# A five-stage graph network on one Trainium2 core: where 832 single-element scatters are issued, and when the first layer compares its edge keys

## The reference, cut to what matters

```
L0: h = gelu(layernorm(conv(h))) + h  four times, then gelu(conv(h))
    conv: alpha = sum(q[dst]*k[src]) / sqrt(32) in 4 heads; softmax over the edges of a dst;
          out = segment_sum(v[src]*attn) + x @ Ws + bs
L1: a relation layer: src_feat = x_rel[type, src], a softmax over each (type, dst), segment_sum
L2: two GCN layers: out = segment_sum(h[src] * dinv[src] * dinv[dst]) + b, an elu between them
L3: out = leaky(segment_sum(edge_weight * h[src]) + b)
x = layernorm(x + L(x)) after each of L0 to L3
```

## Time and profile before

| | |
|---|---|
| runs | 4928.97, 4922.57 and 10345.03 us, median 4928.97 us |
| profiled execution | 4927.95 us, its span 4926.1 us |
| mean granted clock of PE | 0.741 of full speed |
| busy | PE 3395.7, DVE 2708.5, ACT 1597.4, POOL 3350.3 us |
| indirect DMAs of POOL | 1664 + 416 gathers for L0, 416 for L1, 416 + 416 scatters |

### The profile page before, as it was taken

The page is one execution under the profiler, slowest core; times in us unless marked ns, Lnnn a source line. Parts: engine busy times, 40 slices in busy tenths (PEclk is TensorE's granted clock), DMA queues, the critical chain, the costliest instruction groups (busy, mean ns, idle before and its releaser), DMA issues. The chain is left out here.

```text
span 4926.1 us, 76606 instructions
## 1 busy us (share of the span) xinstructions
PE 3395.7 (69%) x17088; PEld 2562.8 (52%) x17089; DVE 2708.5 (55%) x6617; ACT 1597.4 (32%) x3614; POOL 3350.3 (68%) x3343
## 2 busy tenths in 40 slices
PE   6466766676666666656676688885777756969159
PEld 3366653565535555355564566663767653434124
DVE  7577764666646666556665566655777752111001
ACT  5133332334323333223332355562323312221101
POOL 5177766777767777677776777767777767766720
PEclk6677767778777787777867789895555557989579
DMA  8699946666447675376662766643333202323055
GB/s 262 182 274 273 278 143 183 195 202 204 138 140 217 202 206 158 104 219 203 205 182 83 229 202 202 187 117 86 84 69 82 69 11 91 101 91 97 1 204 198
DMA packets 708257, 784.47 MB, mean 159 GB/s; under 512 B 182494, under 2 KB 585924, under 8 KB 704188
## 3 DMA queue, kind: packets, MB, share of 16 engines
q1 hardware_dynamic: 567932, 478.29, 31.4%
q0 software_dynamic: 139968, 302.44, 22.4%
HBM read 657.83 MB, written 122.47 MB: 158 GB/s over the span
## 5 line engine op out<-in xcount | busy, mean ns | idle before, releaser
L673 POOL DMA_INDIRECT kvconv<-kv_tab,src_all x1664 | 1628.4, 979 | 680.3 <-issue 500.0
L2085 POOL DMA_INDIRECT weights<-of_g,cells_g x416 | 454.8, 1093 | 188.1 <-issue 128.0
L687 POOL DMA_INDIRECT counts<-num_now,ord_now x416 | 432.7, 1040 | 193.1 <-issue 154.1
L673 POOL DMA_INDIRECT rows_r<-rel_tab,idx_r x416 | 421.9, 1014 | 141.1 <-issue 125.0
L673 POOL DMA_INDIRECT kvlast<-kv_tab,src_all x416 | 406.1, 976 | 133.5 <-issue 124.4
L1179 ACT ACTIVATE Sconv<-s8conv 128x512 f32<-128x512 fp8e4 x384 | 240.7, 627 | 354.2 <-PE pA1conv L1135 247.1
L1241 DVE TENSOR_TENSOR msgconv<-kvconv,sm_attEconv 128x512 f32<-128x512 f32 x416 | 285.5, 686 | 83.3 <-PE pA0conv L1135 36.5
L1135 PEld LDWEIGHTS pA0conv<-Sconv,msgconv 128*128 128x128 f32 x1664 | 308.6, 260 | 13.8
L1135 PE MATMUL pA0conv<-Sconv,msgconv 128*128 128x128 f32 x1664 | 308.2, 347 | 0.0
L1169 ACT ACTIVATE STconv<-st8conv 128x512 f32<-128x512 fp8e4 x416 | 257.7, 628 | 106.3 <-DMA st8conv<-st_tab 90.6
L1266 DVE TENSOR_REDUCE sm_alphaconv<-prodbconv 128x16 f32<-128x512 f32 x416 | 283.0, 680 | 2.5 <-DVE sm_exconv L526 0.5
(11 more groups left out here) (634 smaller groups left out, 7853.6 us busy)
## 6 DMA issues: line engine op xcount, KB each, us to landing
qwinconv<-q_tab SPq DMA_DIRECT2D x1664, 64.0 KB
raw_g<-counts SPq DMA_DIRECT2D x50, 896.0 KB, 4.8
hot_g<-weights SPq DMA_DIRECT2D x28, 1600.0 KB, 7.5
weights<-blankconv SPq DMA_DIRECT2D x150, 224.0 KB
kvconv<-kv_tab,src_all POOLq DMA_INDIRECT x1664
st8conv<-st_tab SPq DMA_DIRECT2D x52, 512.0 KB
keyrowconv<-key_tab SPq DMA_DIRECT2D x104, 256.0 KB
s8conv<-s_tab SPq DMA_DIRECT2D x52, 512.0 KB
```

Source lines behind the costliest of these rows:

```text
L673: nc.gpsimd.indirect_dma_start(rows[:, par * TG + t, :], None, tab, bass.IndirectOffsetOnAxis(ap=idx[:, g * TG + t:g * TG + t + 1], axis=0 ...
L687: nc.gpsimd.indirect_dma_start(counts, bass.IndirectOffsetOnAxis(ap=ord_now[:, i:i + 1], axis=0), num_now[:, i:i + 1], None).then_inc(sem( ...
L2085: nc.gpsimd.indirect_dma_start(weights, bass.IndirectOffsetOnAxis(ap=cells[:, i:i + 1], axis=0), of[:, i:i + 1], None).then_inc(sem("heavy ...
```

## The change

- Counts: `MID` 26 to 36, `JOINT` 34 to 46, `DRAIN` 30 to 42, and 46 instead of 28 in `last_joint`. That makes 4 x 82 + 88 = 416, so the relation layer scatters no counts any more: neither 5 after each group nor 58 in its drain.
- Weights: 80 are scattered in the drain of the relation layer, after its last gather, from two small buffers that SP fills at the start of that layer (`cells_r`, `of_r`). The other stages get 42 (n1, was 45), 118 (g1, was 110), 34 (e1, was 36), 118 (g2, was 110) and 24 (n2, was 115).
- First layer: `compare`, `matches` and `take` run 8 turns later against the scores than before; `key_rows` and `part_rows` move with them on SP's queue, and the last group's part comes after `sum_rows` in the drain.
- `tables`: POOL writes the iota first, as soon as DVE has read what stood in `first_b`, and gathers then.

```
-JOINT = 34
-MID = 26
+JOINT = 46
+MID = 36
 PER = MID + JOINT
-DRAIN = 30
-EACH = 5
-COUNTED = [(CONVS - 1) * PER, DRAIN + 28, EACH * (GROUPS - 1), T - (CONVS - 1) * PER - DRAIN - 28 - EACH * (GROUPS - 1)]
-WEIGHED = [45, 110, 36, 110, 115]
-MOST = 72
+COUNTED = [(CONVS - 1) * PER, T - (CONVS - 1) * PER]
+DRAIN = 42
+WEIGHED = [80, 42, 118, 34, 118, 24]
+MOST = max(PER, COUNTED[1])
...
                     def _(pool):
+                        pool.wait_ge(ch, 1)
+                        nc.gpsimd.iota(first_b[:, :], pattern=[[1, T]], base=V0, channel_multiplier=0).then_inc(placed, 1)
                         for g in range(2):
                             gather_group(pool, "c_", 0, g, g, kv_tab, src_all, kv)
-                        pool.wait_ge(keyed, 1)
-                        nc.gpsimd.iota(first_b[:, :], pattern=[[1, T]], base=V0, channel_multiplier=0).then_inc(placed, 1)
...
-                            if marks is not None and not (isinstance(g, int) and g * QG + q < 7):
-                                key_rows(g * QG + q - 5, (q + 1) % 2)
-                            if marks is not None and q == 3 and not (isinstance(g, int) and g < 2):
-                                part_rows(g, par)
+                            if marks is not None and not (isinstance(g, int) and g * QG + q < 15):
+                                key_rows(g * QG + q - 13, (q + 1) % 2)
+                            if marks is not None and q == 5 and not (isinstance(g, int) and g < 3):
+                                part_rows(g - 1, 1 - par)
...
                     if marks is not None:
-                        for n in range(GROUPS * QG - 5, GROUPS * QG):
+                        for n in range(LAST * QG - 5, LAST * QG):
                             key_rows(n, n % 2)
                     sp.wait_ge(sem(tag + "S"), quad(LAST - 1, 0))
                     settle(sp)
                     sum_rows(LAST, 0)
+                    if marks is not None:
+                        part_rows(LAST, 0)
+                        for n in range(LAST * QG, GROUPS * QG):
+                            key_rows(n, n % 2)
...
-                            behind = shifted(g, q, par, -1)
+                            behind = shifted(g, q, par, -QG - 1)
...
-                        if marks is not None and q == 1 and started(g):
-                            take(g - 1)
+                        if marks is not None and q == 1 and not (isinstance(g, int) and g < 2):
+                            take(g - 2)
...
-                        if marks is not None and scored(g):
-                            compare(g, q)
+                        if marks is not None and started(g):
+                            compare(g - 1, q)
...
-                    counts_landed(pool, sum(COUNTED[:2]))
+                    counts_landed(pool, T)
...
                     def group(g, par):
                         gather_group(pool, tag, 0, g, par, rel_tab, idx1, rows)
-                        if g == 0:
-                            pool.wait_ge(sem("ord_in"), 32 * (CONVS + 1))
-                        if g < LAST:
-                            add_counts(pool, EACH, EACH * g)
                     gather_all(pool, group)
-                    counts_landed(pool, sum(COUNTED[:3]))
-                    order_in(pool, sum(COUNTED[:3]), COUNTED[3], "ord_pool")
-                    pool.wait_ge(sem("ord_pool"), 32)
-                    add_counts(pool, COUNTED[3])
+                    pool.wait_ge(sem(tag + "weights"), 32)
+                    add_weights(pool, cells, of, 0, WEIGHED[0])
...
                     scatter_rows(0, 0)
-                    order_in(sp, sum(COUNTED[:2]), COUNTED[2])
+                    sp.dma_start(cells[:, :], weigh_at[:, 0:WEIGHED[0]]).then_inc(sem(tag + "weights"), 16)
+                    sp.dma_start(of[:, :], weigh_of[:, 0:WEIGHED[0]]).then_inc(sem(tag + "weights"), 16)
```

More of the change, by code:

```diff
@@ L94, in recycle @@
     def recycle():
-        kept = [n for n in sems if n.startswith(("rows", "settled", "cells", "ord_in", "filled"))]
+        kept = [n for n in sems if n.startswith(("rows", "settled", "cells", "ord_in", "filled", "heavy"))]
         nc.clear_and_free_semaphores([s for n, s in sems.items() if n not in kept])
@@ L1551, in _, with rel_edges @@
                             parts(b - 1)
-        def rel_edges(sb, pb, acc, rs, deg, dinv_f, dinv_n, type_f, mask, last_mask, cuts, idx1):
+        def rel_edges(sb, pb, acc, rs, deg, dinv_f, dinv_n, cells, of, type_f, mask, last_mask, cuts, idx1):
             tag = "r_"
@@ L2271, in _, with late_layers @@
                         v.tensor_scalar(acc[:, cols], pA[b][:, 0:wide(b)], bias, None, ALU.add)
-        def late_layers(l, acc, deg, dinv_f, dinv_n, rs):
+        def late_layers(l, acc, deg, dinv_f, dinv_n, rs, cells, of):
             with ExitStack() as keep:
@@ L2293, in late_layers @@
                         rel_edges(maker(part, nc.sbuf_tensor, "_r"), maker(part, nc.psum_tensor, "_r"), acc, rs, deg,
-                                  dinv_f, dinv_n, *edges)
+                                  dinv_f, dinv_n, cells, of, *edges)
         def elu_joint(tag, acc, y, low, rows, w, bias, dinv_n, pb, weigh, ahead):
@@ L2421, in last_layers @@
                     norm_joint("n1_", acc, rs, sb, pb, [(wb[:, :], w2[1]), (bias[0][:, :], b2[0])], wa, rows=rows,
-                               scale_n=dinv_n, weigh=weigh(0), ahead=counts_ahead("g1_"))
+                               scale_n=dinv_n, weigh=weigh(1), ahead=counts_ahead("g1_"))
                 scope, sb, pb = part("g1_")
                 with scope:
-                    counted("g1_", raw, full, hot, rows, rooted, acc, sb, pb, weigh(1), rs=rs, build=build)
+                    counted("g1_", raw, full, hot, rows, rooted, acc, sb, pb, weigh(2), rs=rs, build=build)
                 scope, sb, pb = part("e1_")
                 with scope:
-                    elu_joint("e1_", acc, y, low, rows, wb, bias[0][:, 0:1], dinv_n, pb, weigh(2), counts_ahead("g2_"))
+                    elu_joint("e1_", acc, y, low, rows, wb, bias[0][:, 0:1], dinv_n, pb, weigh(3), counts_ahead("g2_"))
                 scope, sb, pb = part("g2_")
                 with scope:
-                    counted("g2_", raw, full, hot, rows, rooted, acc, sb, pb, weigh(3),
+                    counted("g2_", raw, full, hot, rows, rooted, acc, sb, pb, weigh(4),
                             loads=[(wc[:, :], w3), (bias[1][:, :], b2[1]), (bias[2][:, :], b3)])
@@ L2434, in last_layers @@
                 with scope:
-                    norm_joint("n2_", acc, rs, sb, pb, [], wc, rows=rows, shift=bias[1][:, 0:1], weigh=weigh(4),
+                    norm_joint("n2_", acc, rs, sb, pb, [], wc, rows=rows, shift=bias[1][:, 0:1], weigh=weigh(5),
                                ahead=weights_ahead)
@@ L2462, in gnn_kernel @@
             acc = scope.enter_context(nc.sbuf_tensor("acc_late", [P, NPAD + P], f32))
+            cells = scope.enter_context(nc.sbuf_tensor("cells_r", [P, WEIGHED[0]], i32))
+            of = scope.enter_context(nc.sbuf_tensor("of_r", [P, WEIGHED[0]], f32))
             with ExitStack() as part:
                 deg = part.enter_context(nc.sbuf_tensor("deg", [1, NPAD + P], f32))
-                late_layers(CONVS - 1, acc, deg, dinv_f, dinv_n, rs)
+                late_layers(CONVS - 1, acc, deg, dinv_f, dinv_n, rs, cells, of)
                 recycle()
```

## The result

The changed kernel takes 4943.64 us, median of 7 runs (4941.83 to 4952.51), against 4922.57 for the kernel before: ratio 1.0045, interval 1.0036 to 1.0055 (one run of the kernel before, at 10345.03 us, does not count in the ratio). That is 0.45% slower, inside the 2% that the forecast named as no difference, but it is a measured loss where I had expected a gain: 4914. The profiled execution took 4943.53 us (span 4941.4), 15.3 us more of span than the one before.

The account below looks back on a forecast made before the run. POOL's string of indirect DMAs was taken to bound the kernel: their unchanged number times their spacing, plus interruptions. Terms summed to -14.1 us against the profiled 4927.95, so 4914, range 4883 to 4947.

Parts of the forecast that it names:

- first drain: First layer's drain: POOL waits some 45 instead of 15.4 us for the later compares and `take`; +29.6, between +22 and +38.
- rival 2: Relation layer: DVE has its own pace, waits for rows become waits for PE, the 44 us do not come; 4958, chance 0.12.
- After it, SP runs as far ahead of DVE as before.: First layer after its first group: SP's lead over DVE unchanged by later key rows; groups 2 to 12 forecast at 0.
- a landing 1.5: End of n2: 24 scatters take 31.2 us and a landing 1.5, against 166.1 us before; -133.4 for n2.
- less 14.53 - 9.80 = 4.7: Last joint: 18 more scatters cost 23.4 us, less 4.7 us of slack in the gap behind it; +18.7.
- Rival 3: A DMA queue still works off earlier scatters, so the 15 us taken off n2 stay; 4929, chance 0.15.
- Relation layer, -26.5 for -35.5: Forecast -35.5: groups -44, gathers' end 44 + 3 us earlier, drain of 80 scatters +25, gap behind it -13.5.
- Rival 1: Relation layer: POOL stays the bound, a group takes some 42 us, up to 32 us more come back; 4882, chance 0.13.
- `MID` and `JOINT`: Conv layers: +10 and +12 scatters at 1.30 us, no slack to fill; 28.6 us a layer, four times, +114.4.
- In front: Tables and first group: -6.3 from the earlier iota and -7.8 from the later key comparison, together -14.1.
- Rival 4: The 118 moved counts cost 1.47 us each beside other work, not 1.30; +20, 4934, chance 0.08.
- Rival 5: First layer: the later key comparison gains nothing in front and only lengthens the drain; +7.8 and up to +8, 4930, chance 0.07.

## Why the prediction was wrong

The number is 29.6 us off (4914 against 4943.6), and three terms make 45 of it; what was missed the other way gives 15 back. That 4943.6 lies within the range of 4883 to 4947 is luck: its upper part stood for a longer first drain and for rival 2, and neither happened.

**The step that failed first: "After it, SP runs as far ahead of DVE as before."** I read the order of waits in the steady state, found it the same, and took the time to be the same. The term for groups 2 to 12 was therefore nothing. The order is the same, and the run with 24 increments shows that nothing in it costs. What changed is that eight compares and a `take` left DVE's code ahead of the loop, which now begins after 471 instructions and not after 490. It then stops 8 us at each of three jumps back, 25 us in all, of which 14.8 reach POOL's gathers. The kernel before with 108 added instructions loses 19 us in those groups, in two smaller stops at each jump.

**The second: "a landing 1.5" in n2, and "less 14.53 - 9.80 = 4.7" in the last joint,** that is, a gap of 9.80 with nothing late behind it. I saw two late landings before, 23.31 and 17.0 us, took both for something of the place, and let both vanish. They belong to column T - 1 of the counts and of the weights. The change moves the count column from the relation layer's drain into the last joint: -12.4 there, near the -13.5 that I had, but +15.0 over the forecast here, which I had not. The weight column stays at the end of n2: +14.9. Rival 3 ("the late landing moves along") had the price and the direction and one of the two places, with the wrong cause. It spoke of a queue still working off long runs; but behind 80 scatters of the relation layer the gap is 10.96 and behind 46 of the last joint 24.63. The rule of the Trainium skill cited there ("DMA: Bandwidth & Descriptors", "Latency and other measured facts": engines 7 and 15 slower under GpSimd's descriptors) does not account for them: with the padding spread over 123 cells and the number of scatters the same, 15.9 us are gone in the last joint and 10.0 in n2. For the 6 us that stay in n2 it is neither shown nor excluded.

**Relation layer, -26.5 for -35.5.** The last gather ends 40.3 us earlier and not 47 (44 for the groups and 3 for the drain's earlier start), at 45.2 us a group; POOL's wait for `msg_r` came, 48.9 us in all. The drain itself took 105 us for 104, and the gap is 10.96, not 9.8. Rival 1 (POOL stays the bound) and rival 2 (the 44 do not come) both fell.

**Right within their bounds:** the first drain (25.8 for 29.6), `MID` and `JOINT` (26.3 a layer instead of 28.6, since in the second layer the gaps at the blocks' ends shrank from 9.80 and 11.33 to 8.98 and 9.81: there were some 2 us of slack that I had denied), `DRAIN`, n1 and e1. Eight columns more in g1 and in g2 were free; their gaps fell from 22.89 and 25.43 to 10.02 and 11.85. In front the gain was 18.2 for 14.1. Rival 4 (1.47 a scatter) fell: the added ones cost 1.24 in `MID` (47.4 us for 36, 35.0 for 26), 1.29 in `JOINT` (61.1 for 46, 45.7 for 34) and 1.31 in the last joint (64.8 for 46, 41.2 for 28). Rival 5 fell: the later comparison does bring 9.9 us in front.

As a plan the change is still no gain. Taken together (estimated from the two runs, not run as one), without the loop's stops and the padding's lateness it would stand near 4942 - 15.5 - 23.5 = 4903, and the kernel before without that lateness ran at 4892.86.

## What to carry to other kernels

When what waits for a string of DMAs is released far later than the last one's end would suggest, look at what that one writes before looking at queues. Padding that all goes to one cell cost 10 to 16 us here each time it was waited for; it should go to separate cells, or be followed by other work, and then not stand right ahead of loads that someone waits for. After an edit, look at the first instruction of every rolled loop for idle time released by "issue"; an edit far ahead of a loop can move it to a place where each jump back costs 4 or 8 us, and a few idle instructions in front of it are a test that takes one run. And a gap that one change should remove has to be tied to its cause first, since it may be carried along.

## What the runs showed of the hardware

**Jumps back.** DVE's first loop, by the number of DVE's instructions ahead of it in the compiled program: 471: stops of 7.8 to 9.0 us (four traces); 490 and 495: none; 579: one stop of 3.6 to 4.9; 598: two, 2.7 to 5.5 each. The Trainium skill ("Runtime: NRT & Kernel Launch", "Instruction fetch mechanics") says that instructions are fetched ahead in blocks of 256, of which an engine other than PE holds two, and that a taken branch to outside them stalls for a fetch. The first three places agree with it for this loop of 311 instructions if a block begins between 471 and 490, which no run shows, and I chose 108 by it so that both loops should lie in two blocks; the runs with 108 say otherwise, 4.86 and 3.03 us. That the stops depend on the place is shown; by what rule stays open, and that they are fetches is the page's reading, not something that these rows name.

**One cell.** A scatter of 128 elements of which 123 write one cell keeps its waiters longer than the same scatter with separate cells: 15.9 us for the 2-byte counts (24.63 against 8.78 behind the last joint) and 10.0 us for the 4-byte weights (17.3 against 7.3 in n2). By these differences a further write to the cell costs an estimated 0.08 to 0.13 us.

**A pause in long strings.** In every run POOL stands still for 3.0 us before the 114th weight scatter of a block that has so many: in g1 and g2 of the changed kernel, in n2 of the kernel before. The gathers, 416 in a block, show nothing like it; nothing here tells why.
